# Eight of thirty-two elementwise LayerNorm operations issued on GpSimd instead of VectorE

## The reference

```python
xn = (x - mean(x)) / sqrt(var(x) + 1e-5)              # over the features
q, k, v = xn @ Wq.T, xn @ Wk.T, xn @ Wv.T             # 16 heads of 128
attn = softmax(q @ k.T * 128**-0.5) @ v @ Wo.T
base = xn @ W_base.T + b_base
e = argmax(xn @ router_W.T)                           # one of 8 experts per token
delta = (xn @ A.T, kept for expert e alone) @ Bw * 2
y = x + attn + base + delta
```

## Time and profile before

| | |
|---|---|
| median of 3 runs | 1305.62 us (1302.56 to 1306.41) |
| the profiled execution | 1299.51 us |
| its span, slowest core (core 1) | 1298.0 us |
| spans of the 8 cores | 1288.7 to 1298.0 us |
| granted TensorE clock, mean of core 1 | 0.974 |
| TensorE matmul busy | 1130.7 us (87%) |
| VectorE busy | 397.9 us (31%) |
| GpSimd busy | 100.4 us (8%) |

### The profile page before, as it was taken

How to read it: one execution, slowest core, us unless ns; L and a number is a source line. 1 busy time by engine, 2 the same in 40 slices (tenths; PEclk the granted TensorE clock), 3 DMA queues, 4 the chain that set the end, 5 groups by cost and what they waited for, 6 DMA issues and landing times.

```text
span 1298.0 us, 14702 instructions; the slowest of 8 cores (1288.7 to 1298.0 us)
## 1 busy us (share of the span) xinstructions
PE 1130.7 (87%) x5266; PEld 471.3 (36%) x5266; DVE 397.9 (31%) x489; ACT 486.8 (38%) x419; POOL 100.4 (8%) x96
## 2 busy tenths in 40 slices
PE   4624889898999999999999999999999999989997
PEld 1102434343434343433333333333333333334433
DVE  2367540404040303131313131313131313144445
ACT  4510162625253535353534343434444444440000
POOL 1200201010101010101010101010101010001110
PEclk9867999999999999999999999999999999999999
DMA  8950593333334242424151515151515150307996
GB/s 244 284 57 1 73 106 33 33 34 33 35 30 37 30 40 25 44 23 47 19 48 18 49 18 49 17 49 17 50 17 49 17 49 1 33 1 130 171 196 184
DMA packets 174773, 77.56 MB, mean 60 GB/s; under 512 B 168432, under 2 KB 168432, under 8 KB 172656
## 3 DMA queue, kind: packets, MB, share of 16 engines
q0 software_dynamic: 168656, 51.42, 37.7%
q1 hardware_dynamic: 3744, 16.82, 4.6%
q10 hardware_dynamic: 2304, 8.39, 1.6%
HBM read 111.26 MB, written 8.39 MB: 92 GB/s over the span
## 4 chain that ended last, share of the span: by engine, by line
PE 70%; DMA 11%; ACT 9%; DVE 5%; issue 4%; ACTq 0%; POOL 0%; DVEq 0%; SPq 0%; POOLq 0%
PE PD L611 9%; PE PC L598 9%; PE PC L545 8%; PE PD L651 8%; PE PA L585 8%; PE PB L478 8%; PE PA L478 8%; DMA arena<-x 7%; PE PB L525 4%; ACT arena L532 4%; DMA y<-arena 4%; PE PA L525 3%; DVE xn_s L378 1%; DVE xn_s L363 1%; ACT arena L668 1%
## 5 line engine op out<-in xcount | busy, mean ns | idle before, releaser
L540 DVE TENSOR_TENSOR arena<-arena 128x1024 bf16<-128x1024 bf16 x240 | 166.2, 693 | 219.7 <-ACT arena L532 219.7
L545 PE MATMUL PC<-arena 128*128 128x512 bf16 x512 | 151.6, 377 | 55.7 <-ACT arena L532 32.9
L532 ACT ACTIVATE arena<-PB,consts 128x1024 bf16<-128x1024 f32 x128 | 153.9, 1203 | 53.3 <-PE PB L525 38.7
L532 ACT ACTIVATE arena<-PA,consts 128x1024 bf16<-128x1024 f32 x128 | 154.3, 1206 | 35.5 <-PE PA L525 35.3
L651 PE MATMUL PD<-xn_s,arena 128*128 128x512 bf16 x512 | 139.0, 378 | 0.0
L569 ACT CAST arena<-PA 128x1024 bf16<-128x1024 f32 x16 | 16.2, 1012 | 276.0 <-PE PB L478 221.2
L585 PE MATMUL PA<-xn_s,arena 128*128 128x512 bf16 x480 | 106.0, 379 | 12.5 <-ACT arena L569 12.5
L611 PE MATMUL PD<-xn_s,arena 128*128 128x512 bf16 x512 | 113.1, 379 | 0.0
L598 PE MATMUL PC<-xn_s,arena 128*128 128x512 bf16 x512 | 113.1, 379 | 0.0
L478 PE MATMUL PB<-xn_s,arena 128*128 128x512 bf16 x480 | 106.0, 379 | 0.0
L478 PE MATMUL PA<-xn_s,arena 128*128 128x512 bf16 x480 | 106.0, 379 | 0.0
(11 more groups left out here) (110 smaller groups left out, 906.3 us busy)
## 6 DMA issues: line engine op xcount, KB each, us to landing
arena<-x SPq DMA_DIRECT2D x8, 1024.0 KB, 7.9
arena<-x POOLq DMA_DIRECT2D x8, 1024.0 KB, 8.0
arena<-wk POOLq DMA_DIRECT2D x16, 512.0 KB, 11.2
arena<-wq POOLq DMA_DIRECT2D x16, 512.0 KB, 9.3
arena<-wv POOLq DMA_DIRECT2D x16, 512.0 KB, 7.4
arena<-x SPq DMA_DIRECT2D x16, 512.0 KB, 6.2
arena<-wb POOLq DMA_DIRECT2D x16, 512.0 KB, 7.5
arena<-wo POOLq DMA_DIRECT2D x16, 512.0 KB, 9.3
```

What stands on the lines that cost most here:

```text
L532: return s.activation(p_sb[:, (tkc % 2) * SO:(tkc % 2 + 1) * SO], src[:, 0:SO], AF.Exp, bias=ck("shift"), scale=ck("scale"))
L540: return v.tensor_add(dst, dst, pc_)
L545: last = t.matmul(PC[:, o0:o0 + w], lhsT=vt_sb[:, tkc * 128:(tkc + 1) * 128], rhs=p_sb[:, (tkc % 2) * SO + o0:(tkc % 2) * SO + o0 + w], st ...
```

## The change

The subtraction of chunks 3, 7, 11 and 15, and the multiplication of chunks 2, 6, 10 and 14, are emitted to GpSimd's queue. The operations, their operands and what they wait for stay as they are. No chunk has both of its operations on GpSimd. In GpSimd's queue the eight stand behind the DMA issue of `bw` (L345) and ahead of the weights of the heads.

```diff
@@ -361,7 +361,8 @@
         def emit_sub(c):
             def sub_m(v, c=c):
                 return v.tensor_sub(xn(c), xn(c), mb_s)
-            p.emit("vector", sub_m, reads=["mb", f"xn{c}"], writes=[f"xn{c}"])
+            eng = "gpsimd" if c % 4 == 3 else "vector"
+            p.emit(eng, sub_m, reads=["mb", f"xn{c}"], writes=[f"xn{c}"])
...
@@ -376,7 +377,8 @@
         for c in range(nD):
             def mul_r(v, c=c):
                 return v.tensor_mul(xn(c), xn(c), rb_s)
-            p.emit("vector", mul_r, reads=["rb", f"xn{c}"], writes=[f"xn{c}"])
+            meng = "gpsimd" if c % 4 == 2 else "vector"
+            p.emit(meng, mul_r, reads=["rb", f"xn{c}"], writes=[f"xn{c}"])
```

## The result

The changed kernel took 1325.37 us (median of 10 runs), the one before beside it 1305.71 us (10 runs). The ratio is 1.0157, with a 95% interval of 1.0133 to 1.0181: slower by 20.5 us (17.4 to 23.6). The ratio is taken over the fast runs alone (one of each ten is slow), so it differs a little from that of the medians. The forecast was +28.4 us, 1334.0 us, with a range of 1312 to 1348. Direction and mechanism were right, the size was 8 us too large.

A forecast was written before the change was run, and what follows sets the result against it. TensorE bounds the whole kernel, but VectorE this stage; +30.6 us from GpSimd taking turns with VectorE, less 2.2 in the loop, gives +28.4: 1327.9 us against the profiled execution, 1334.0 as median, range 1312 to 1348 us.

The forecast's parts named there:

- They exclude each other: VectorE instructions with two SBUF inputs and GpSimd instructions reading SBUF take turns; otherwise a 5.6 us gain was expected.
- P: Time of one moved operation on GpSimd, taken as 4.54 us, between 1.14 and 6.8; each microsecond is 8 us.
- Steps 1 to 3: Ahead of `rb`: GpSimd's four subtractions take turns with VectorE's work, so the cast L369 comes 15.7 us late.
- Step 4: From `rb` to multiplication 1's end: GpSimd's four multiplications take turns with VectorE, 18.2 - 3.4 us added.
- Step 5: Rest of the loop: no GpSimd work left, chunks multiplied earlier fall to TensorE's 1.50 us, gaining 2.2 us.
- starts cold in both kernels: TensorE's clock at the start of its work: the same in both kernels, so nothing was added.
- After the stage: After 145 us: weight slices about as late as everything behind the loop and no later; the kernel only shifts.
- A: Rival for the whole stage: the two engines don't exclude each other, -5.6 us, 1300.0 us; chance 9%.
- B: Rival for the whole stage: VectorE goes first, GpSimd gets only what it leaves, +7 us, 1313 us; chance 8%.
- C: Rival for the whole stage: they exclude each other but P is 1.14 to 2.3 us, +1 to +10 us; chance 6%.

The follow-up runs named there:

- memset kernel: Changed kernel with each of GpSimd's eight operations replaced by a 128x6144 f32 memset of a free region, reading nothing; ratio to before 0.9985, stage 62.6 us.
- run with the wait: Changed kernel with GpSimd's subtractions 7, 11 and 15 each waiting for the end of the one before; 1324.48 us, where the kernel before took 1306.99.

## Why the prediction was right, point by point

**They exclude each other: right.** This was the choice on which the sign hung, made where no row showed the pair. L351's 16.84 us and 3.85 us for each operation among VectorE's subtractions show the exclusion, and the memset kernel shows its condition: beside a VectorE operation with two inputs, GpSimd has to read. The overlap in the earlier trace rows was true and no counter-example, as an issue reads no tile. But the rows that tipped the choice were of another kind: in the earlier trace rows operations of VectorE with one input wait for, or hold up, issues that read no tile, much as the cast held up the memset by 0.9 us, where the two-input operations and the memsets passed each other. To that extent the choice was right by more than its rows could show. The Trainium skill (SBUF — State Buffer, "Who interferes with whom") has a rule for the pair that was added: a VectorE instruction with two SBUF inputs contends with a GpSimd instruction that reads SBUF, not with one that only writes it. These traces agree with both halves (L351 16.84 us beside the subtractions, 2.27 beside the memsets).

**P: the term that was mis-sized.** 4.54 us was estimated, 4.01 us measured from one of GpSimd's subtractions to the next (16.05 for four). Eight times 0.53 is 4.2 us, about half of what the forecast was off. The two ends, 1.14 and 6.8, held it. How the estimate was made (two inputs read one after the other, each at VectorE's f32 pace) is not shown: a copy with one input cost VectorE 1.69 us, and twice that is 3.4, not 3.85. The upper end of the range, 1348 us, belongs to a P of 6.3, not 6.4. The Trainium skill's 4497 ns (GPSIMD Engine Reference, "Performance versus the Vector engine") is for f32; for bf16 the measurement decides, and it is shorter.

**Steps 1 to 3, ahead of `rb`: right in size, wrong in order.** +15.7 was forecast, +14.5 measured, on every core. The turns did not alternate. GpSimd did its four subtractions in one piece, then L351 and L353 followed, and Exp, not VectorE, released the cast at 103.06. The prediction's own steps with P at 4.0 give the cast at 104.1, +13.5: the piece of four cost 1.0 us more than turns, and P 2.2 less, so one error hid part of the other. That the size ahead of `rb` came out within 1.2 us is in part luck. The run with the wait showed that an order with turns was there to be had, and 5.5 us better.

**Step 4, behind `rb`: right in its order, too large by P.** +14.8 was forecast. Measured, `rb` to the end of multiplication 1 is 136.94 - 109.04 = 27.9 us, where it was 112.43 - 96.54 = 15.9: +12.0, which is 4 x 3.85 - 3.4, in place of 4 x 4.54 - 3.4. Multiplication 14 fell between 0 and 1, as worked out.

**Step 5, the loop: mis-sized.** 2.2 us was the gain forecast; from the end of multiplication 1 to the first reduction it is 28.7 us in place of 32.8: 4.1. The chunks with GpSimd's multiplication do take 1.50 us (1.49 from router matmul to router matmul). The other 1.9 us come from the first chunk, whose matmuls at the low clock take 2.9 us. Before, multiplication 1 ended 1.9 us ahead of the end of these matmuls, so TensorE held the stage up for that long; now they lie under the wait for multiplication 1. With the multiplications alone, number 14 fell ahead of 0, nothing hid them, and that kernel's stage is 1.8 us longer than 4 x 3.85 - 4.1 had it. Saying that TensorE "starts cold in both kernels" missed that it starts cold under a wait. It missed a smaller thing the other way too: on six of the eight cores of the changed kernel one or two chunks behind the first still ran at the low clock (2.7 to 2.9 us each), and their stages are 90.9 to 92.0 us, where the other two, the profiled one among them, have 89.9.

**After the stage: as forecast.** The weights follow the mask's reduction as before (166.16 us, 0.50 behind the reduction's start at 165.66; before, 0.43), and everything behind shifts. On the two profiled cores the stage's +22.4 us (14.5 + 12.0 - 4.1) stands against +20.5 (17.4 to 23.6) in the runs. So of the 8 us that the forecast was off, 1.2 lie ahead of `rb`, 2.8 behind it and 1.9 in the loop; the other 2 are within the interval of the runs.

**The rivals.** A failed on the reads: its -5.6 us came out as -5.4 only where GpSimd wrote and didn't read. B has something for it, the three subtractions that went through ahead of a waiting GpSimd in two of the other kernels, but in the changed kernel VectorE waited 14.6 us at L351. C failed on P, 3.85 to 4.0 us where it had at most 2.3.

## What to carry to other kernels

Before work is moved to an idle engine, ask what the two engines share, and compare an instruction's length under overlap with its usual length; such waits are counted as busy and stand in no list of waits. GpSimd was worth something here only under work of VectorE that reads PSUM or waits: one operation there gained 1.5 us, eight elsewhere cost 23. Ask also what the loop waits for: emitting one small addition behind the multiplication in place of ahead of it gained 6.1 us of the stage, about what the change could have gained at its best.

## What the runs showed of the hardware that wasn't expected

An engine whose next operation is ready can keep its turn over several: GpSimd over four (16.05 us, with VectorE waiting), VectorE over three beyond the one that it was in (GpSimd waiting 5.3 us), though in other places the waiting one got in after one. A memset of one column in between changed nothing (L351 16.95 us), a wait for GpSimd's own last result did (4.84 us). The exclusion isn't limited to VectorE's two-input operations: the one-input cast of the reciprocal root, 1.22 us alone, took 4.02 us behind a subtraction of GpSimd and 1.86 behind a copy, and held up even a memset (6.12 us in place of 5.22), while VectorE's casts from PSUM kept their 1.22 us beside GpSimd's subtraction. And the low clock ends at different moments on cores that run the same program: in the changed kernel the stage is 89.9 us on one core and 92.0 on another, whose clock was still 0.50 for two chunks more (rows of that core):

```profile
137.50:139.50 2.00, 2.00 (x13) 0.90 (x12) 0.59 (x2) 0.00 (x0) 0.00 (x0) 0.50 0.00 0
139.50:141.50 2.00, 2.00 (x13) 0.82 (x11) 0.76 (x1) 0.00 (x0) 0.00 (x0) 0.54 0.00 0
141.50:143.50 2.00, 1.71 (x18) 0.74 (x16) 1.36 (x2) 0.00 (x0) 0.00 (x0) 1.00 0.03 8
```
